# A quantised last stage: another order of ScalarE's, GpSimd's and TensorE's operations in a step, and the late scale computed on ScalarE

## The reference

```python
def act_quant(x):
    scale = 127.0 / jnp.clip(jnp.max(jnp.abs(x), axis=-1, keepdims=True), 1e-05)
    return jnp.clip(jnp.round(x * scale), -128, 127) / scale
def bit_linear(x, w):                       # weight_quant: -1, 0 or 1, over a scale
    return jnp.einsum('bsd,hd->bsh', act_quant(x), weight_quant(w))
h = bit_linear(x, w1)                                        # 128 -> 512
h = depthwise_conv1d(h.transpose(0, 2, 1), conv_w, conv_b)   # 3 taps over the positions
h = jax.nn.silu(h.transpose(0, 2, 1))
return bit_linear(h, w2)                                     # 512 -> 128
# in the layer: x = x + tanh(g_ffn[1]) * that(_layernorm(x))
```

## Time and profile before

| | |
|---|---|
| time, median of 3 runs | 1009.33 us (999.88 to 1013.99) |
| the profiled execution | 1009.39 us, span 1007.6 us |
| busy share of the span | PE 95%, DVE 84%, ACT 74%, POOL 58% |
| POOL's busy share, slices 33 to 39 of 40 | 8 tenths (the quantised stage) |
| granted TensorE clock, mean over the span | 0.988 |

### The profile page before, as it was taken

How to read it: one execution, slowest core, us unless ns; L and a number is a source line. 1 busy time by engine, 2 the same in 40 slices (tenths; PEclk the granted TensorE clock), 3 DMA queues, 4 the chain that set the end, 5 groups by cost and what they waited for, 6 DMA issues and landing times.

```text
span 1007.6 us, 36351 instructions
## 1 busy us (share of the span) xinstructions
PE 958.8 (95%) x11842; PEld 743.9 (74%) x11842; DVE 846.0 (84%) x2411; ACT 741.9 (74%) x1653; POOL 584.5 (58%) x1230
## 2 busy tenths in 40 slices
PE   6999999999999999999999999999999899999997
PEld 2777777777789999998877676767776666777775
DVE  5888888889689989888887888888877789999997
ACT  4877787788687777775657777777778777777774
POOL 6454554545125556656886535454554288888884
PEclk9999999999699999999999999999999999999999
DMA  3401010100000000000000000000000000000001
GB/s 108 176 24 42 21 42 31 32 21 11 13 2 2 0 0 0 0 0 1 2 12 24 13 22 10 21 10 12 19 11 2 2 15 21 21 21 21 21 21 30
DMA packets 19359, 21.49 MB, mean 21 GB/s; under 512 B 3552, under 2 KB 12000, under 8 KB 19296
## 3 DMA queue, kind: packets, MB, share of 16 engines
q1 hardware_dynamic: 19296, 20.68, 6.6%
HBM read 16.48 MB, written 4.19 MB: 21 GB/s over the span
## 4 chain that ended last, share of the span: by engine, by line
PE 30%; POOL 13%; issue 7%; ACT 2%; DVE 1%; POOLq 1%; ACTq 0%; DVEq 0%
PE bank L1276 8%; PE bank L1299 6%; POOL ln_rs L271 4%; PE score L1353 4%; POOL hid_b L555 3%; PE bank L1414 2%; PE score L1345 2%; PE bank L1323 2%; POOL xdq L551 2%; PE bank L1315 1%; PE bank L1311 1%; PE bank L1318 1%; ACT prob_t L581 1%; POOL ln_nr L271 1%; POOL ln_ve L271 1%
## 5 line engine op out<-in xcount | busy, mean ns | idle before, releaser
L581 ACT ACTIVATE prob_t<-bank 128x512 f32<-128x512 f32 x256 | 152.8, 597 | 124.9 <-PE bank L1276 116.8
L923 DVE TENSOR_REDUCE smax<-score 128x16 f32<-128x1024 f32 x128 | 156.8, 1225 | 49.1 <-PE score L1353 38.0
L1276 PE MATMUL bank<-const,prob 128*128 128x128 f32 x1024 | 167.7, 287 | 15.7 <-ACT prob_t L581 15.7
L1299 PEld LDWEIGHTS bank<-vb,prob_t 128*64 128x64 f32 x4096 | 131.6, 139 | 50.3 <-issue 42.2
L932 DVE TENSOR_TENSOR prob<-score,smax 128x512 f32<-128x512 f32 x256 | 164.9, 686 | 1.3
L576 ACT ACTIVATE prob<-prob 128x512 f32<-128x512 f32 x256 | 161.2, 630 | 6.1 <-DVE prob L932 5.4
L1276 PEld LDWEIGHTS bank<-const,prob 128*128 128x128 f32 x1024 | 109.4, 142 | 69.9 <-issue 60.7
L1299 PE MATMUL bank<-vb,prob_t 128*64 128x18 f32 x4096 | 144.4, 213 | 0.0
L411 POOL TENSOR_SCALAR kj<-k_sb,const 128x512 f32<-128x512 f32 x128 | 88.1, 695 | 74.8 <-issue 46.3
L656 ACT ACTIVATE eb_t<-eb,gwt 128x128 f32<-128x128 f32 x256 | 81.4, 390 | 45.2 <-POOL eb_acc L454 29.0
L382 POOL TENSOR_TENSOR a_ve<-a_mv,const 128x4 f32<-128x4 f32 x32 | 6.5, 203 | 147.9 <-DVE a_mv L925 143.8
(11 more groups left out here) (157 smaller groups left out, 2378.7 us busy)
## 6 DMA issues: line engine op xcount, KB each, us to landing
ctx_t<-in_ctx SPq DMA_DIRECT2D x32, 256.0 KB, 2.6
x_all<-in_x SPq DMA_DIRECT2D x16, 256.0 KB, 2.8
out_x<-x_all SPq DMA_DIRECT2D x64, 64.0 KB, 1.5
ew<-in_ew SPq DMA_DIRECT2D x2, 512.0 KB, 5.8
f_cw<-in_f_cw SPq DMA_DIRECT2D x1, 768.0 KB, 7.7
w_t<-in_w_attn SPq DMA_DIRECT2D x2, 256.0 KB, 3.8
f_w<-in_f_w SPq DMA_DIRECT2D x2, 256.0 KB, 6.5
eb<-in_L_ffn_eb SPq DMA_DIRECT2D x1, 256.0 KB, 6.5
```

The lines of the kernel that those rows point to most:

```text
L581: act.activation(prob_t[:, 4 * half:4 * half + 4, :].rearrange("p i q -> p (i q)"), bank[PT], ACT.Copy).then_inc(s["p_copied"], 1)
L923: dve.tensor_reduce(smax[:].rearrange("p (r h) -> p r h", r=RH), sc, AX.X, ALU.max).then_inc(s["smax_done"], 1)
L1276: return pe.transpose(dst, src, ident)
L1299: last = pe.matmul(bank[OV][q, i * 2 * VW:(i + 1) * 2 * VW], prob_t[:, i, q], vb[:, k // G, v0 + b * NPAIR + i, :, :].rearrange("p h v -> ...
```

## The change

- **ACT** (ScalarE): `q2t` of tile t-4 goes from the head of the step to behind `quantise`. A new operation, `late_scale`, computes `sc_l` of tile t-3 (a copy of one column with a scale from a column) behind it.
- **POOL** (GpSimd): the order `tap_lo`, `xdq`, `q2` becomes `tap_lo`, `q2`, `xdq`. The wait for `q1` now stands ahead of `xdq` alone, and each of the three has waits of its own.
- **PE** (TensorE): the transpose of tile t+2 goes ahead of the four products of tile t-4.
- **DVE** (VectorE): `sc_l` is no longer computed there. The sum into `x_all` and `sc_i` wait for the semaphore that ScalarE now raises; `sc_i` had that wait before.

```diff
--- before.py
+++ after.py
@@ -532,28 +532,26 @@
                 o = 1 - par
                 if has(4):
                     ln_rstd(pool, t + 4, par)
+                if has(1):
+                    wait(pool, "conv_mm", t)
+                    wait(pool, "xhi_copied", t + 2)
+                    pool.tensor_tensor(shifted(tap_lo, o, 1), x_t[:, o, :], shifted(tap_hi, o, 1), ALU.subtract)\
+                        .then_inc(s["xlo_done"], 1)
+                if has(-2):
+
+                    in_registers(pool, t + 3, t - 3)
+                    pool.wait_ge(s["const_in"], 16)
+                    wait(pool, "sc_ready", t + 3)
+                    wait(pool, "q2_int", t - 3)
+                    pool.tensor_scalar(q2[:, par, :], hact[:, par, :], sc_q[:, o, 1:2], ROUND, ALU.mult, ALU.add)\
+                        .then_inc(s["q2_ready"], 1)
                 if has(2):
 
+                    in_registers(pool, t + 3)
+                    pool.wait_ge(s["const_in"], 16)
                     wait(pool, "q1_done", t + 3)
-                else:
-                    if has(-2):
-                        wait(pool, "sc_ready", t + 3)
-                        wait(pool, "q2_int", t - 3)
-                    if has(1):
-                        wait(pool, "xhi_copied", t + 2)
-                        wait(pool, "conv_mm", t)
-                if has(1):
-                    if isinstance(t, int):
-                        wait(pool, "xhi_copied", t + 2)
-                    pool.tensor_tensor(shifted(tap_lo, o, 1), x_t[:, o, :], shifted(tap_hi, o, 1), ALU.subtract)                        .then_inc(s["xlo_done"], 1)
-                if has(2):
-
                     pool.tensor_scalar(xdq[:, par, :], q1[:], -ROUND, sc_i[:, o, 0:1], ALU.add, ALU.mult)\
                         .then_inc(s["xq_ready"], 1)
-                if has(-2):
-
-                    pool.tensor_scalar(q2[:, par, :], hact[:, par, :], sc_q[:, o, 1:2], ROUND, ALU.mult, ALU.add)\
-                        .then_inc(s["q2_ready"], 1)
 
             lead_in(ffn, -4, -3)
             tap_lower()
@@ -793,15 +791,23 @@
                 act.activation(x_t[:, par, :], bank[FRONT][:, 0:P], ACT.Copy)
                 act.activation(shifted(tap_hi, par, 1), bank[FRONT][:, 0:P], ACT.Copy).then_inc(s["xhi_copied"], 1)
 
+            def late_scale(t, par):
+                wait(act, "sc_v", t + 5)
+                wait(act, "x_out", t - 1)
+                act.activation(sc_l[:, par:par + 1], sc_i[:, 1 - par, 1:2], ACT.Copy, scale=f_s[:, 6:7])\
+                    .then_inc(s["sc_late"], 1)
+
             def ffn(t, par, has):
+                if has(-1):
+                    silu(t - 1, 1 - par)
+                if has(2):
+                    quantise(t + 2, par)
                 if has(-4):
                     wait(act, "q2_tr", t - 3)
                     wait(act, "out_mm", t - 5)
                     act.activation(q2t[:, par, :], bank[PT], ACT.Copy).then_inc(s["q2_copied"], 1)
-                if has(-1):
-                    silu(t - 1, 1 - par)
-                if has(2):
-                    quantise(t + 2, par)
+                if has(-3):
+                    late_scale(t - 3, 1 - par)
                 if has(4):
 
                     ln_apply(act, t + 4, par, "q1_done", t + 3)
@@ -1206,6 +1212,7 @@
                         .then_inc(s["q2_int"], 1)
                 if has(-5):
                     wait(dve, "out_mm", t - 4)
+                    wait(dve, "sc_late", t - 4)
                     dve.scalar_tensor_tensor(out=x_tile(t - 5), in0=bank[6][:, 0:P], scalar=sc_l[:, o:o + 1],
                                              in1=x_tile(t - 5), op0=ALU.mult, op1=ALU.add).then_inc(s["x_out"], 1)
                 if has(5):
@@ -1229,9 +1236,6 @@
                     wait(dve, "conv_mm", t + 1)
                     wait(dve, "silu_done", t - 1)
                     dve.tensor_tensor(hpre[:, par, :], bank[par], f_cb[:], ALU.add).then_inc(s["hpre_done"], 1)
-                if has(-3):
-                    wait(dve, "x_out", t - 4)
-                    dve.tensor_scalar(sc_l[:, o:o + 1], sc_i[:, par, 1:2], f_s[:, 6:7], None, ALU.mult).then_inc(s["sc_late"], 1)
                 if scales:
 
                     if has(-1):
@@ -1571,6 +1575,8 @@
                     wait(pe, "xlo_done", t + 1)
                     for tap in range(TAPS):
                         conv_tap(par, tap)
+                if has(2):
+                    transpose_xq(t + 2, par)
                 if has(-4):
                     wait(pe, "q2_copied", t - 3)
                     wait(pe, "x_out", t - 4)
@@ -1578,8 +1584,6 @@
                         last = pe.matmul(bank[6][:, 0:P], q2t[:, par, c * P:(c + 1) * P], f_w2t[:, c, :],
                                          start=(c == 0), stop=(c == FC - 1))
                     last.then_inc(s["out_mm"], 1)
-                if has(2):
-                    transpose_xq(t + 2, par)
                 if has(-3):
                     wait(pe, "q2_int", t - 2)
                     wait(pe, "q2_copied", t - 3)
```

## The result

| | before | after |
|---|---|---|
| median of 6 runs each | 1001.45 us (999.88 to 1013.99) | 989.37 us (988.76 to 992.32) |
| profiled execution | 1009.39 us | 992.32 us |
| its span, mean granted clock | 1007.6 us, 0.988 | 990.5 us, 0.997 |
| sixth transpose of `xdq` to the last (58 steps) | 812.17 to 992.67, 3.112 a step | 804.72 to 975.93, 2.952 a step |
| last transpose to the end of the span | 14.93 us | 14.60 us |

The ratio after to before is 0.9851, with a 95% interval of 0.9807 to 0.9894: faster, by less than 2%. (The quotient of the two medians is 0.988, inside that interval.) The forecast was 995.5 us with a range of 986 to 1005.

What follows compares the result with a forecast made beforehand. A round trip of 3.10 us a step in the last stage bounds the kernel; afterwards PE's 2.84 plus 0.04 gives 2.88. 58 x 0.23 = 13.3 us and 0.6 in the drain off 1009.39 give 995.5 us, range 986 to 1005.

Steps and rivals of the forecast that it cites:

- The round trip of 3.10: Quantised last stage, transpose of `xdq` around to the next: sets the pace; without `q2t` (0.49) and `tap_lo` (0.40) 2.21 us.
- PE: 2.76 + 0.08 = 2.84: TensorE's step: 2.60 plus 0.16 for the transpose, plus 0.08 for the loop's end; sets the pace after.
- GpSimd: mostly 2.73: GpSimd's own load a step, 2.58 to 2.87 depending on `ln_rs`; new waits taken as 0.
- The rival "less": GpSimd slowed by VectorE's work, needing 2.99 to 3.04 a step: 1002 to 1005 us; chance 0.15.
- ScalarE, and the late scale at 0.3: ScalarE's load 2.6 a step, at most 2.8, under PE's 2.84, with 0.3 us taken for the late scale.
- The added waits cost nothing: `sc_i` starts about 2.07 after the silu, the late scale ends at most 1.97 after: no cost, narrowly.
- VectorE: 2.65, under PE: VectorE's step 2.91 less 0.34 for `sc_l`, 2.57, plus 0.08 for the loop: 2.65.
- The path over the convolution, + 0.04: Last convolution product over `hpre` to the next step's transpose, 2.79; slack about 0.25, so 0.04 a step added.
- The sum: 2.88 a step against 3.11: 58 x 0.23 = 13.3 us, plus 0.6 in the drain, off 1009.39: 995.5 us.
- The signs: Trace marks for right or wrong; wrong included PE waiting for `xdq` as before or a pace of 3.0 and more.
- Slower: `q2b` held by `q2`: VectorE's `q2b` waits for GpSimd's `q2`, 0.69 each step: 3.34 a step, 1022 us; chance 0.05.

Runs made afterwards that it cites:

- b2: Kernel before with only `q2t` moved behind `q1` on ScalarE; late scale stays on VectorE: pace 2.953 us a step, median 996.59 us, ratio to before 0.992.
- b1: Kernel before with ScalarE's part only (its new order and the late scale): pace 2.837 us a step, median 992.21 us, ratio to before 0.986.
- c2: Changed kernel with `xdq` ahead of `q2` on GpSimd, each keeping its own waits: pace 2.768 us a step, median 979.27 us, ratio to before 0.977.
- c1: Changed kernel with `ln_mv` ahead of the maximum over the hidden values on VectorE: pace 2.881 us a step, median 987.89 us, ratio to before 0.986.
- a1: Changed kernel with the late scale computed on VectorE again: pace 3.072 us a step, median 1004.82 us.
- c4: The changed kernel run again without further edit: pace 2.944 us a step, median 991.70 us, ratio to before 0.989.

## Why the prediction was right, and where it wasn't

The time lies in the range, and a change of less than 2% was called the likeliest. The mechanism named for before held; the one named for after did not. The number came near by luck: the gain in the steps was put 4 us too high, the base some 8 us too high, and the two errors partly cancel.

- **The round trip of 3.10 sets the pace before, and falls.** Right: b2 takes only the 0.49 of `q2t` out of it, and the pace drops by 0.16. Both cuts together were more than needed: b1 leaves `tap_lo` behind `q1` and has a better pace than the change.
- **PE: 2.76 + 0.08 = 2.84.** Too high. The regular step is 2.70, since the transpose adds 0.11 (908.19 to 908.30) and not 0.16; with 0.2 at a pass's end c2 runs at 2.77. I took the 0.16 from a transpose whose weights had waited.
- **GpSimd: mostly 2.73.** Too low, though `ln_rs` itself came out shorter than in the earlier trace rows:

```profile
L271 POOL TENSOR_TENSOR ln_rs<-ln_ve,const x64: 550/556/839, 765.3 to 968.0; 128x1 f32<-128x1 f32 x64
```

  From `xdq` to `xdq` without a wait GpSimd took 2.97 (898.98 to 901.95) and 2.79 (the next step), and in c1 its pace was 2.89. The rival "less" was this mechanism and priced it at 2.99. In after it is one step of the four in the chain, and with the wait for `ln_mv` gone it is what decides (c1, 2.88).
- **ScalarE, and the late scale at 0.3.** Right: it took 0.286 in the mean (277 to 303 ns, 64 times), and ScalarE is busy 2.47 a step. The estimate of 0.28 by the Trainium skill (ScalarE: Activation LUTs, "What ACT_TABLE_LOAD costs") agrees with that number.
- **The added waits cost nothing.** Right: no wait of `sc_i` or of the sum for the late scale is in the list of waits.
- **VectorE: 2.65, under PE.** True of its load (2.62), and misleading. I used the removed `sc_l` only as load. It is worth more as a link: a1 gives 3.072 with it and 2.952 without, 0.12 a step or 7 us of the change's 9.3.
- **The path over the convolution, + 0.04.** This is the step that failed. I followed it as convolution, `hpre`, silu, `q1`, `xdq`, one step long, and priced its meeting with GpSimd's `ln_rs` at 0.04. The path that decides leaves `hpre` along VectorE's order, to `ln_mv`, over the norm and GpSimd's order to `xdq` of a later tile, and in most of the stage over one more step of GpSimd's: 11.85 us in four steps, 2.96 where I had 2.88. Against what PE needed by itself in c2, 2.77, the two together cost 0.18 a step where I had 0.04.
- **The sum.** 58 x 0.23 = 13.3 was forecast, 9.3 came; the drain gave 0.33 for 0.6. That the time was below the forecast and not above it comes from the base: 1009.39 held the stretch at clock 0.91. From the median of all six runs, 1001.45, my steps would have given 987.6, and the ones measured give 991.8, against the 989.37 (and in c4 991.70) that were timed. The lower end given for the forecast, 986, doesn't follow from its pace of 2.80 either: 58 x 0.31 = 18.0 and at most 2.4 for the drain end at 989.
- **The signs.** One that was named for "wrong" stands in the rows: TensorE waits for `xdq` as much as before, 17.3 + 1.8 us in the list of waits of after against 11.6 + 4.1 before.
- **Slower: `q2b` held by `q2`.** Not in this form: in after no `q2` was ahead of a `q2b` that it met, and it was `tap_lo` that stood ahead of the longest `q2b` (0.69 for 0.43, at 959.83). Such ones stay rare; the mean is 0.452. By the rule of the Trainium skill (SBUF — State Buffer, "Who interferes with whom"), which it gives for VectorE's modes with two ports, who is second is blocked until the first is through. Here `q2` at 906.67, 0.06 behind a `q2b` of 0.43, took 0.93, that is 0.24 more, and the `q2b` kept its 0.43; the earlier trace rows had 0.81. By the rule it would be the 0.37 that `q2b` had left. VectorE's next operation begins at 906.95, 0.28 behind the start of `q2`, so the rows agree in who pays and nearly in how much. Here the profile shows it as a longer second operation and not as a later start; whether `q2b` runs in such a mode, no row tells.

## What to carry to other kernels

When a round trip is cut, the next bound needs not be an engine: look for chains that close only after several steps, by following the waits of the changed order backwards until the same wait comes again, and divide by the steps in between. Count how often the wait occurs: here it was one step in four, and three steps that looked like the whole loop left out one of GpSimd's own. An operation on an engine with spare time still costs time if it stands between two hand-overs of the chain (0.34 on VectorE: 0.12 a step); so order each engine by what is waited for (`xdq` ahead of `q2`, `ln_mv` ahead of a maximum) before moving work to other engines. Take the base of a sum from the median of several runs and see whether its profile holds a stretch of lower clock.

## What the runs showed of the hardware

- VectorE and GpSimd slow each other in small and large operations alike (a duration on GpSimd is rough by itself, but the starts agree: `xdq` follows the `q2` of 906.67 after 0.90, and that of 901.28, which took 0.69, after 0.67). From the tiles of after, 840 to 960 us (count, min/median/max ns):

```profile
L1211 DVE TENSOR_SCALAR q2b<-hid_b x41: 425/427/691, 840.8 to 959.8; 128x512 bf16<-128x512 f32 x41
...
L546 POOL TENSOR_SCALAR hid_b<-hid_b,sc_q x40: 684/692/932, 841.9 to 957.5; 128x512 f32<-128x512 f32 x40
```

  Each is longer by 0.24 to 0.26 at most. Between `q2b` and `tap_lo` or `q2` it is the second that pays; `ln_rs` pays although it was first:

```profile
852.36 0.84 POOL L271 TENSOR_TENSOR ln_rs<-ln_ve,const 128x1 f32<-128x1 f32 x1
...
852.74 0.43 DVE L1211 TENSOR_SCALAR q2b<-hid_b 128x512 bf16<-128x512 f32 x1
...
959.82 0.42 POOL L538 TENSOR_TENSOR tap_lo<-x_t,tap_hi 128x128 fp32r<-128x128 f32 x1
959.83 0.69 DVE L1211 TENSOR_SCALAR q2b<-hid_b 128x512 bf16<-128x512 f32 x1
```

  Over the whole stage `ln_nr`, a 128x1 operation of 0.19, took up to 0.48. The sum changes little with the order: where `ln_rs` is spared (0.70 to 0.60 in the mean), `q2`, `ln_nr` and `tap_lo` pay (0.69 to 0.74, 0.19 to 0.26, 0.41 to 0.44).
- A wait for a semaphore that is already there cost nothing that the rows show on GpSimd: its new order has three groups of waits and register instructions in place of one, and with them it ran as tight as before (in c2 `q2` starts at 900.73, 0.36 after an `xdq` that lasts 0.37).
- The end of a pass costs VectorE 0.31 (3.4/11) and TensorE 0.24 (2.6/11), and the pace gets only part of it back when there are half as many: passes of eight gave 0.045 a step on the change and 0.05 on b1.
